# The router of a mixture-of-experts block: logits turned by plain transposes, their halves added by GpSimd, the sigmoid one inner step later

## The reference

```python
logits = h @ gate_w                      # [2048, 512] @ [512, 32]
scores = jax.nn.sigmoid(logits)
sfc = scores + e_bias[None, :]
group_scores = jnp.sum(jax.lax.top_k(sfc.reshape(T, G, E // G), 2)[0], axis=-1)
_, gidx = jax.lax.top_k(group_scores, TKG)          # 2 of 4 groups
...
_, topk_idx = jax.lax.top_k(sfc_masked, K)          # 4 experts
topk_w = jnp.take_along_axis(scores, topk_idx, axis=1)
topk_w = topk_w / (jnp.sum(topk_w, axis=-1, keepdims=True) + 1e-20) * SCALE
```

## Time and profile before

| | us |
|---|---|
| median of 3 runs | 1069.31 (1068.93 to 1069.31) |
| the profiled execution | 1067.82 |
| its span, first to last instruction | 1066.1 |
| PE busy in the span | 1050.9 (99%) |
| DVE / ACT / POOL busy | 592.4 / 543.1 / 433.1 |

### The profile page before, as it was taken

One profiled execution on the slowest core, in us unless ns is written; L12 is line 12 of the kernel. 1 busy time (PEld: TensorE's weight loads), 2 busy tenths in 40 slices (PEclk: granted clock), 3 DMA queues, 4 the chain that ended last, 5 costly groups with the idle time before them and its releaser, 6 DMA issues.

```text
span 1066.1 us, 17311 instructions
## 1 busy us (share of the span) xinstructions
PE 1050.9 (99%) x4894; PEld 846.6 (79%) x4895; DVE 592.4 (56%) x1114; ACT 543.1 (51%) x893; POOL 433.1 (41%) x328
## 2 busy tenths in 40 slices
PE   7999999999999999999999999999999999999998
PEld 3456888888888888888887888888888888888886
DVE  7987947904580467041017697945555555555514
ACT  5553546333333333333345344367777777777742
POOL 1031303321122122211223433477788777888642
PEclk9999999999999999999999999999999999999999
DMA  8605296516421642334255691178988899888666
GB/s 281 234 1 197 87 337 208 178 60 240 157 98 60 241 157 94 101 127 152 95 218 184 251 313 52 36 193 172 263 201 217 216 235 294 170 160 164 78 209 274
DMA packets 97604, 186.66 MB, mean 175 GB/s; under 512 B 15496, under 2 KB 34952, under 8 KB 97168
## 3 DMA queue, kind: packets, MB, share of 16 engines
q1 hardware_dynamic: 78304, 150.58, 41.1%
q0 software_dynamic: 18816, 34.64, 17.0%
q10 hardware_dynamic: 432, 0.79, 0.3%
HBM read 137.78 MB, written 58.98 MB: 185 GB/s over the span
## 4 chain that ended last, share of the span: by engine, by line
PE 92%; DVE 6%; issue 1%; ACT 0%; POOL 0%; DMA 0%; SPq 0%; DVEq 0%; ACTq 0%; POOLq 0%
PE bank L635 41%; PE bank L958 24%; PE bank L1573 14%; PE bank L539 5%; PE bank L1565 3%; PE bank L1581 2%; PE bank L969 1%; PE bank L979 1%; PE bank L1028 1%; DVE bns L321 1%; DVE bns L251 0%; POOL mix_lo L375 0%; DMA f<-in_L_attn_x 0%; DVE hb L804 0%; DVE f L354 0%
## 5 line engine op out<-in xcount | busy, mean ns | idle before, releaser
L939 POOL TENSOR_TENSOR ksp_lo<-ra,ksp_hi 128x512 fp32r<-128x512 f32 x96 | 141.7, 1476 | 444.4 <-ACT ksp_hi L889 444.3
L1573 PE MATMUL bank<-w,xT 128*128 x672 | 158.8, 379 | 0.8 <-ACT xT L1639 0.8
L958 PE MATMUL bank<-vring,ksp_hi 128*128 128x512 f32 x512 | 159.5, 393 | 0.0
L1721 DVE TENSOR_TENSOR wd_lo<-w,wd_hi 128x1024 fp32r<-128x1024 f32 x84 | 103.0, 1226 | 80.4 <-ACT wd_hi L1656 80.4
L881 ACT ACTIVATE ra<-bank 128x512 f32<-128x512 f32 x96 | 57.4, 598 | 175.1 <-PE bank L635 172.8
L1573 PEld LDWEIGHTS bank<-w,xT 128*128 128x128 f32 x672 | 127.3, 190 | 20.5 <-issue 1.1
L635 PE MATMUL bank<-wd_hi,aT 128*128 128x512 f32 x336 | 125.8, 415 | 0.0
L889 ACT ACTIVATE ksp_hi<-ra 128x512 fp32r<-128x512 f32 x96 | 60.7, 632 | 120.3 <-PE bank L958 119.8
L958 PEld LDWEIGHTS bank<-vring,ksp_hi 128*128 128x128 f32 x512 | 95.6, 188 | 19.9
L635 PE MATMUL bank<-xcT_hi,wck_lo 128*128 128x512 f32 x256 | 101.8, 398 | 0.0
L635 PE MATMUL bank<-xcT_lo,wck_hi 128*128 128x512 f32 x256 | 101.6, 397 | 0.0
(11 more groups left out here) (274 smaller groups left out, 2048.1 us busy)
## 6 DMA issues: line engine op xcount, KB each, us to landing
vring<-wcv_d SPq DMA_DIRECT2D x64, 512.0 KB, 3.3
w<-in_L_ffn_Wu SPq DMA_DIRECT2D x32, 512.0 KB, 6.6
w<-in_L_ffn_Wd SPq DMA_DIRECT2D x32, 512.0 KB, 7.2
hT_d<-hT SPq DMA_DIRECT2D x16, 512.0 KB, 4.2
hTb<-hT_d SPq DMA_DIRECT2D x3, 2048.0 KB, 11.8
raw_wcv<-in_L_attn_Wcv SPq DMA_DIRECT2D x4, 1024.0 KB, 6.7
raw_wck<-in_L_attn_Wck SPq DMA_DIRECT2D x4, 1024.0 KB, 9.4
f<-in_L_attn_x SPq DMA_DIRECT2D x4, 1024.0 KB, 6.9
```

The lines of the kernel that those rows point to most:

```text
L939: nc.gpsimd.tensor_tensor(ksp[1][:, i % 2], ra[:, i % 2], ksp[0][:, i % 2], ALU.subtract).then_inc(sem("klo_in"), 1)
L958: m = nc.tensor.matmul(bank[to + j][:], ksp[l][:, i % 2, j * P:(j + 1) * P], rhs(r), start=i == 0 and k == 0, stop=i == last and k == 2)
L1573: m = nc.tensor.matmul(bank[4 + u][:, 0:EI], xT4[:, u, c * P:(c + 1) * P], slot_of(wu8[:, :, c * EI:(c + 1) * EI], e), start=c == 0, stop= ...
L1721: nc.vector.tensor_tensor(lo, slot_of(wd8, e), hi, ALU.subtract).then_inc(sem("wl4"), 1)
```

## The change

The stacked identities `pair` and the DVE instruction that made them are gone. `pe_scores` now transposes each [64, 128] piece of `lgT` with a 64x64 identity: bank 6 then holds 256 columns, for each tile 32 sums of the upper and 32 of the lower halves. Behind step 5, ACT copies them to the new tile `lsum` (in place of the sigmoid). POOL adds the halves (`pool_logits`). ACT takes the sigmoid from `lsum` behind its work of step 6. POOL's loop in stage 2 starts at block 1, with block 0 written out ahead of it; the addition of the last block stands in stage 3 ahead of `pool_numbers`. PE waits for one `gwlo` where there were two. Line numbers of the changed kernel are a few higher.

```diff
@@ -163,7 +163,7 @@
         gw = at("gw", [P, C, 2, E], R, 180.5)
         gwf = at("gwf", [P, C, E], F, 181.5)
         lgT = at("lgT", [2 * E, BLK], F, 182)
-        pair = at("pair", [2 * E, E], F, 184.25)
+        lsum = at("lsum", [P, BT, 2, E], F, 184.25)
         tmp = at("tmp", [P, BT, H], F, 186)
         scores = at("scores", [P, NT, E], F, 194)
 
@@ -824,7 +824,6 @@
             dve_lo(dve, "wck0")
             dve.wait_ge(sem("gwhi"), 1)
             nc.vector.tensor_tensor(gw[:, :, 1], gwf[:], gw[:, :, 0], ALU.subtract).then_inc(sem("gwlo"), 1)
-            nc.vector.tensor_tensor(pair[:], ident[0:2 * E, 0:E], ident[0:2 * E, E:2 * E], ALU.add).then_inc(sem("gwlo"), 1)
             for j in range(BT):
                 nc.vector.tensor_tensor(xx(0, j), xx(0, j), f2[:, j], ALU.add).then_inc(sem("sum0_in"), 1)
             dve.wait_ge(sem("sum0_in"), BT)
@@ -908,8 +907,10 @@
                 act_hi_h(act, b, 3)
             if i == TH_AT + 2:
                 wait_apart(act, sem("tsc_in"), b + 1)
-                nc.scalar.activation(scores[:, bass.ds(b * BT, BT)].rearrange("p j e -> p (j e)"), bank[6][:, 0:BT * E],
-                                     ACT.Sigmoid).then_inc(sem("sc_in"), 1)
+                nc.scalar.activation(lsum[:].rearrange("p j s e -> p (j s e)"), bank[6][:, 0:BT * 2 * E], ACT.Copy).then_inc(sem("lslo_in"), 1)
+            if i == TH_AT + 3:
+                wait_apart(act, sem("lsum_in"), b + 1)
+                nc.scalar.activation(scores[:, bass.ds(b * BT, BT)], lsum[:, :, 0], ACT.Sigmoid).then_inc(sem("sc_in"), 1)
 
         EARLY = {0: "wcv2", 1: "wck1", 2: "wck2", 3: "wck3", 5: "wcv3"}
 
@@ -933,6 +934,11 @@
                 act_block2(act, b)
             act_block2(act, NB - 1, last=True)
 
+        def pool_logits(pool, b):
+
+            wait_apart(pool, sem("lslo_in"), b + 1)
+            nc.gpsimd.tensor_tensor(lsum[:, :, 0], lsum[:, :, 0], lsum[:, :, 1], ALU.add).then_inc(sem("lsum_in"), 1)
+
         def pool_inner(pool, n, i):
 
             pool.wait_ge(sem("khi_in"), n + 1)
@@ -940,9 +946,13 @@
                                     ALU.subtract).then_inc(sem("klo_in"), 1)
 
         def stage2_gpsimd(pool):
-            with pool.Fori(0, NB) as b:
+            for i in range(NCI):
+                pool_inner(pool, i, i)
+            with pool.Fori(1, NB) as b:
                 for i in range(NCI):
                     pool_inner(pool, b * NCI + i, i)
+                    if i == TH_AT + 2:
+                        pool_logits(pool, b - 1)
 
         def pe_inner_up(pe, n, i, weights, rhs, kc=4):
 
@@ -1010,7 +1020,8 @@
 
             wait_apart(pe, sem("sg_in"), b + 1)
             for j in range(BT):
-                m = nc.tensor.matmul(bank[6][:, j * E:(j + 1) * E], lgT[:, j * P:(j + 1) * P], pair[:], start=True, stop=True)
+                m = nc.tensor.transpose(bank[6][:, j * 2 * E:(j + 1) * 2 * E], lgT[:, j * P:(j + 1) * P],
+                                        ident[0:2 * E, 0:2 * E])
             m.then_inc(sem("tsc_in"), 1)
 
         def pe_turn_xc(pe, b, c):
@@ -1062,7 +1073,7 @@
         def stage2_tensor(pe):
             pe.wait_ge(sem("wlo"), split_count("wcr"))
             pe_block2(pe, 0, first=True)
-            pe.wait_ge(sem("gwlo"), 2)
+            pe.wait_ge(sem("gwlo"), 1)
             with pe.Fori(1, NB - 1) as b:
                 pe_block2(pe, b)
             pe_block2(pe, NB - 1, last=True)
@@ -1247,6 +1258,7 @@
                 if first and i in LATE3:
                     lo3(pool, nc.gpsimd, ORDER3[LATE3[i]])
                 if first and i == TH_AT + 2:
+                    pool_logits(pool, NB - 1)
                     pool_numbers(pool)
                 if last and i == NSI - 2:
                     first_gathers(pool, 0, 3)
```

## The result

| kernel | executions | median | lowest to highest | ratio to before |
|---|---|---|---|---|
| before | 6 | 1068.37 | 1067.28 to 1069.31 | |
| changed | 6 | 1073.76 | 1071.54 to 1082.35 | 1.0052 [1.0033, 1.0070] |

The changed kernel is slower by 0.5%, about 5.5 us (3.5 to 7.5 by the interval). The range of 1070.2 to 1075.0 holds it; the likeliest case (1071.9, its own range up to 1073.0) does not. The profiled execution of the changed kernel took 1071.54 with a span of 1069.8, 3.7 above that of before. It is the fastest of its six, so the profile can show only about 3.7 of the 5.5. The slowest of the six, 1082.35, had a mean granted clock of 0.946 where the other five had 0.997 or 0.998.

The account below looks back on a forecast made before the run. PE, busy 99% of the span, was taken as the bound. A 5.0 us wait for the late routing less 2.4 us from shorter scores gave +2.6 us, 1071.9 from 1069.31; the range was 1070.2 to 1075.0.

Parts of the forecast that it names:

- rival (a): PE's clock falls while it stands for the cast; half pace afterwards costs about 2.5 us more, 1074.4; chance 0.22.
- PE's gain: Scores on PE, four blocks: plain transposes replace f32 matmuls, 0.60 us less per block, -2.4 us in all.
- Rival (c): Transposes on PE are no cheaper, each piece still two records; no gain, 1074.3; chance 0.05.
- ACT and POOL in stage 2: Copy, second small activation and POOL's addition, under 2 us per block on engines with idle time, cost nothing.
- The sigmoid's time: Last block: ACT's sigmoid ends at 600.20 behind step 6; DVE starts 0.1 later, 600.30 instead of 593.99.
- The leg: DVE's routing from sigmoid to the cast releasing `sel_in`: bare 15.95 us plus 4.1 for meetings with POOL.
- Rival (b): DVE's leg meets no POOL instruction; stall only 0.9 us, change not slower, 1067.8; chance 0.10.
- The wait: PE, ready for the count matmuls at 615.36, stands 5.0 us for the cast (bounds 0.9 and 6.1).
- Behind the counts: After the count matmuls PE and DVE go on with PE's shift; DVE's extra 1.7 us fits its 7.76 idle.
- Forecast 0.60: The main case, wait less gain with no fall of the clock: +2.6 us, 1071.9; chance 0.60.
- the sign that the prediction had named: PE's records behind the counts doubling in duration would show the forecast wrong.
- Carried to the median as they are: The sum of wait and gain, +2.6 us, was added directly to the median 1069.31, giving 1071.9.

Follow-up runs that it names:

- r0: The changed kernel again, unaltered, timed beside the kernel before: 1074.33, ratio 1.0059.
- r8: Changed kernel with POOL's two subtractions of steps 0 and 1 of stage 3's block 1 waiting for the routing's cast: 1073.35, ratio 1.0037.
- r5: Changed kernel with the last block's addition on POOL ahead of its weight half and the last sigmoid back in step 5: 1067.84, ratio 1.0003.
- r6: Changed kernel, but in the last block DVE adds the halves and the sigmoid is back in step 5: 1068.65, ratio 1.0000.
- r2: Changed kernel with the count matmuls one inner step later, behind step 2 of stage 3's block 1: 1068.17, ratio 0.9996.
- r4: Kernel before with only the sigmoid moved, behind step 6 instead of step 5: 1076.22, ratio 1.0065.
- r9: Changed kernel with the sigmoid another step later, behind step 7, and POOL's numbers behind its subtraction of step 7: 1077.77, ratio 1.0083.
- r1: Changed kernel with 18 extra matmuls into a free bank ahead of the count matmuls, filling PE's wait: 1071.88, ratio 1.0029.
- r3: Kernel before with the transposes alone, halves not added, sigmoid in its old place on the upper halves only: 1067.15, ratio 0.9986.
- r7: r6 with the count matmuls in step 2, as in r2: 1067.70, ratio 0.9992.
- r10: The kernel of r7 measured again on another occasion: 1067.65, ratio 0.9984.

## Why the prediction was right, and where it was wrong

The time lies in the range, but the forecast's own sum does not give it: +2.6 forecast, +5.4 measured. The range holds it because it was stretched to rival (a). In the profiled execution (+3.7) the wait was 4.7 (5.0 forecast) and the gain 2.8 (2.4), the clock put 1.4 on top (2.5 in r0) and a second wait 0.3; what the median has beyond that stays open.

**PE's gain, right.** 0.60 per block forecast, 0.61 measured; a record has 222 ns, and the four of a block stand in the chain with 0.39 rather than 1.01. Rival (c) is out: one record per transpose.

**ACT and POOL in stage 2, right.** The shift falls by the same 0.61 a block, so nothing waits for the new work. POOL's addition took 0.47, between the bounds.

**The sigmoid's time, right; DVE's start 0.3 late.** In the new trace's time the sigmoid was to end at 600.20 - 2.77 = 597.43, and ended at 597.06 + 0.29 = 597.35. DVE began 0.50 later and not 0.1 (below, on the hardware), at 597.85 where 600.30 - 2.77 = 597.53 was forecast. `ksp_lo` of step 6 came behind the numbers at 599.06, and PE never waited for it there.

**The leg, right.** 19.32 against 20.05, meetings 3.3 against 4.1 (one by one 0.97, 1.12, 0.26 and 0.94 against 1.2, 1.1, 0.6 and 1.2). The bare leg was taken 0.1 too short: three operations of 64 columns that meet nothing take 0.90 with the gaps between them (changed kernel, 601.78), not 0.81. The meetings stand where `ksp_lo` ran, and r8 took two of them away by holding POOL off. Rival (b) is out. The Trainium skill, "SBUF — State Buffer", section "Who interferes with whom", adds that casts and scalar operations of VectorE, which have one input, can also take the shared ports in their fast modes. I had read it for two-input operations alone; the trace agrees, r5 and r6 show the cast at 1.37 against 0.43. No run held POOL off the cast, so that its 0.94 is the port's is argued. It is one reason why putting the sigmoid back did not free PE of the wait; the other is that PE itself comes sooner.

**The wait, right.** 5.0 forecast, 4.7 measured.

**"Behind the counts", a second wait of PE: missed.** The forecast had both engines go on with PE's shift. PE waited 0.2 us for `ksp_lo` at the end of block 1 and lost 0.3 by it (r2: 0.55 and 0.7), one of the signs that the prediction itself had named.

**"Forecast 0.60", no fall of the clock: wrong.** Rival (a), with 0.22, is what happened in both profiled executions of the changed kernel, in r4, r8 and r9. The records behind the counts took 0.63 us in place of 0.39 and started 0.42 apart (618.98 to 619.40) in place of 0.23, the sign that the prediction had named, and r1 shows that the clock is the cause. The step that failed is "Against it: the new wait is shorter than 6.7, and PE comes to it from full work". The first of the rows showed one wait behind which the engine was slow, and I took its length for something like a bound without a row between 1.25 us (no fall) and 6.7 us that would have borne that out. Waits of 3.37 and 4.57 do it as well, and full work ahead of them is no protection. Rival (a)'s price of 2.5 is the upper end of what the runs show (1.36, 1.44, 1.59, 1.62, 2.53). The Trainium skill, "TensorE: Matmul & The Clock Gate", section "HAM oscillation — how this bites in real kernels", reckons the loss as half of the throttled time. The runs agree roughly, if only the time counts in which PE works (5.4 us and 2.53 in r0, 2.9 and 1.36 in r9, where 6.8 us were throttled in both).

**"Carried to the median as they are": partly wrong.** Even r1, without a fall, is at +3.2 [2.0, 4.1] where its starts show +1.9 at the first `down`; r2, r3 and r7 are 0.7 to 1.7 above what theirs show. The slips in stage 4 are of that size. Whether a changed time of PE makes them more frequent, or whether the single profile of before (1067.82, 0.4 to 1.3 below the medians of before) happened to have none, is not settled. The execution of 1082.35 wasn't profiled; its low mean clock, 0.946, is all that is known of it.

## What to carry to other kernels

Before a step is moved past its neighbours, compare the move with the slack at the next meeting: 6.3 us of delay against 1.74 of slack lose more than four savings of 0.6 us bring, and a faster bounding engine shrinks that slack as well. If the engine that bounds is left standing for some us, add to the wait the slow stretch behind it; work that is thrown away (r1) removes that stretch, and a later place for the waiting instruction (r2, r7) removes both. A late chain can still cost at its next meeting (r2). In a chain of small vector operations, look at what GpSimd does beside each, casts included.

## What the hardware showed that I had not expected

The granted clock can fall behind much shorter waits. In stage 1 PE waits for ACT's `f` each time. In r7, and in the kernel before:

```profile
20.37 8.68 PE L539 MATMUL bank<-dec,f 128*128 128x512 f32 x16 [2.50 <-ACT f L421]
```

```profile
20.37 7.13 PE L539 MATMUL bank<-dec,f 128*128 128x512 f32 x16 [1.25 <-ACT f L421]
```

Behind 2.50 us of idle the same sixteen records took 8.68 in place of 7.13, at a clock of 0.50 from 20.1 to 23.5; r6 (2.58), r8 (2.21), r9 (2.08) and r10 (2.01) show it too, while the other eight profiles (0.87 to 1.70) kept 1.00. `f` comes at 20.1 to 20.7 us in all; how long PE waits for it depends on how soon PE was fast behind its first idle time. In r7, and in the kernel before:

```profile
6.54 11.33 PE L599 MATMUL bank<-g1b,onesq 128*128 128x512 f32 x22 [6.54 <-DMA g1b<-in_L_attn_ln_b]
```

```profile
6.68 12.44 PE L599 MATMUL bank<-g1b,onesq 128*128 128x512 f32 x22 [6.68 <-DMA g1b<-in_L_attn_ln_b]
```

These 22 records took 11.13 to 11.49 us in the five profiles with a fall and 11.67 to 12.66 in the other eight. So the length of the wait and the moment from which PE was fast go together, and the rows don't show which of them decides. The fall cost little there: PE's next wait for `f`, 0.8 us in the eight, is gone in the five, and at 269 us the five are 0.1 to 0.5 behind the kernel before, the others between level and 0.3 ahead.

Second, the fall need not come during the wait: in r8 the clock was still 1.00 when PE restarted and fell some 0.9 us later, under full work. Third, the same wait of 4.57 was followed by 3.4 us at half clock in two executions (changed, r4) and by 6.8 us in a third (r0), which alone moves this kernel's time by 1.1 us. Fourth, from the start of the last sigmoid to DVE's first routing row there are 0.79 or 0.80 us in changed, r0, r1, r2, r5, r8 and r9 (597.06 to 597.85 in the rows above), 0.35 to 0.37 in before, r3 and r4 (593.62 to 593.99 in the earlier trace rows) and 0.39 or 0.40 in r6, r7 and r10, though the sigmoid's own row is as long everywhere (0.26 to 0.31). In the first seven it reads what POOL has added, in r6, r7 and r10 what DVE has added, in the others the bank. What makes the 0.4 wasn't tried.
